# Waiting for a quarter of the input at a time in the first norm, and two bulk transfers issued ahead of the third layer norm

## What is computed

```python
x = hidden_states                                   # [16, 256, 128]
xn = layernorm(x)
s = L0_attn(xn)                                     # starts with an RMS norm of xn, then a gated linear recurrence and an MLP
g = silu(L0_ffn(xn))                                # two layers of local attention and feed-forward
x = x + s * g
xn = layernorm(x)                                   # "third layer norm": call 3 of the kernel
s = L1_attn(xn)                                     # 16 heads, ALiBi bias, causal
g = silu(L1_ffn(xn))                                # mixture of experts, 8 experts, each token goes to its best one
x = x + s * g
# two more layers of the same form: rope attention + ternary MLP, latent attention + linear map in the frequency domain

def L1_ffn(x):
    top1 = argmax(x @ Wg + bg)
    h = relu(x @ W1[top1] + b1[top1])
    return h @ W2[top1] + b2[top1]
```

## Time and profile before

| | |
|---|---|
| median of 3 runs | 2362.21 us (2360.13 to 2365.6) |
| the profiled execution | 2350.24 us, its span 2348.4 us |
| mean granted TensorE clock in it | 0.915 of full speed |
| PE busy | 1970.9 us, 84% of the span |
| DVE busy | 1403.9 us, 60% |
| ACT busy | 1173.3 us, 50% |
| POOL busy | 729.9 us, 31% |
| first matmul | 13.42 us |
| third layer norm | 1087.68 to 1126.95 us |
| alibi attention with routing | from 1126.95 us; the experts' first transfer is issued at 1394.29 |

### The profile page before, as it was taken

The page is one execution under the profiler, slowest core; times in us unless marked ns, Lnnn a source line. Parts: engine busy times, 40 slices in busy tenths (PEclk is TensorE's granted clock), DMA queues, the critical chain, the costliest instruction groups (busy, mean ns, idle before and its releaser), DMA issues. The chain is left out here.

```text
span 2348.4 us, 68942 instructions
## 1 busy us (share of the span) xinstructions
PE 1970.9 (84%) x28845; PEld 1250.0 (53%) x28845; DVE 1403.9 (60%) x2804; ACT 1173.3 (50%) x1869; POOL 729.9 (31%) x759
## 2 busy tenths in 40 slices
PE   5577899996959999787699989458998957999997
PEld 1232577763326777532555559325555414667765
DVE  5544788753568887255577735547775054556562
ACT  5663466654526666464366644325666441333333
POOL 0202666741057666201233103522220013222220
PEclk8787899998979999898699989759999987899999
DMA  3000000000000000000545520223441012433441
GB/s 136 0 0 1 2 3 3 3 3 1 0 1 3 3 3 3 2 0 5 160 121 128 137 60 28 77 57 95 98 99 43 0 41 91 133 124 119 139 127 39
DMA packets 93704, 122.43 MB, mean 52 GB/s; under 512 B 9376, under 2 KB 80384, under 8 KB 90048
## 3 DMA queue, kind: packets, MB, share of 16 engines
q1 hardware_dynamic: 91352, 113.84, 17.3%
q0 software_dynamic: 2048, 4.20, 0.6%
HBM read 67.62 MB, written 49.15 MB: 50 GB/s over the span
## 5 line engine op out<-in xcount | busy, mean ns | idle before, releaser
L1671 ACT ACTIVATE at_pr<-ps 128x768 f32<-128x768 f32 x256 | 203.9, 811 | 92.4 <-PE ps L1572 86.9
L1060 POOL TENSOR_TENSOR la_tc<-la_ta,la_tb 128x512 f32<-128x512 f32 x128 | 162.7, 1271 | 112.2 <-DVE la_tb L1356 108.2
L1077 PE MATMUL ps<-w_l0f,la_hs 128*128 128x512 f32 x256 | 152.7, 681 | 47.0 <-DVE la_tb L1356 40.7
L1996 ACT ACTIVATE at_pr<-ps 128x640 f32<-128x640 f32 x128 | 90.0, 703 | 179.4 <-PE ps L1899 179.4
L2038 DVE TENSOR_REDUCE at_m<-ps 128x2 f32<-128x512 f32 (+3 forms) x256 | 113.4, 485 | 105.7 <-PE ps L1899 102.1
L1716 DVE TENSOR_REDUCE at_m<-ps 128x2 f32<-128x512 f32 x256 | 174.2, 680 | 0.0
L2289 POOL TENSOR_TENSOR at_parts<-at_ta,at_tb 128x512 f32<-128x512 f32 x64 | 81.2, 1269 | 246.7 <-DVE at_tb L2279 242.7
L1047 POOL TENSOR_TENSOR la_qn<-la_tc,la_rn 128x512 f32<-128x512 f32 x128 | 133.9, 1046 | 52.9 <-issue 36.9
L1715 DVE TENSOR_REDUCE at_m<-ps 128x2 f32<-128x256 f32 x256 | 107.7, 421 | 67.2 <-PE ps L1572 62.7
L1572 PE MATMUL ps<-cast 64*64 64x256 bf16 x2048 | 146.3, 276 | 0.0
L1354 DVE TENSOR_TENSOR la_ta<-ps,la_tab 128x512 f32<-128x512 f32 x128 | 88.2, 689 | 95.7 <-ACT la_sq L1280 95.7
(11 more groups left out here) (380 smaller groups left out, 4872.9 us busy)
## 6 DMA issues: line engine op xcount, KB each, us to landing
scratch_latent<-at_parts SPq DMA_DIRECT2D x32, 640.0 KB
at_qs<-scratch_latent SPq DMA_DIRECT2D x32, 320.0 KB
at_ks<-scratch_latent SPq DMA_DIRECT2D x32, 320.0 KB
scratch_alibi<-at_parts SPq DMA_DIRECT2D x32, 192.0 KB
at_ks<-scratch_alibi SPq DMA_DIRECT2D x32, 192.0 KB
scratch_rope<-at_parts SPq DMA_DIRECT2D x32, 192.0 KB
at_ks<-scratch_rope SPq DMA_DIRECT2D x32, 192.0 KB
w_l0f<-in_l0f SPq DMA_DIRECT2D x2, 1689.5 KB, 15.6
```

Of the source, the lines that this page charges most:

```text
L1060: nc.gpsimd.tensor_tensor(tc[:, x, :], ta[:, x % 2, :], tb[:, x % 2, :], ALU.add).then_inc(s.la_tc, 1)
L1077: nc.tensor.matmul(ps[:, 0, :], hs[:, i % QSLOTS, t * P:(t + 1) * P], w("wq" if p < 2 else "wk"), start=True, stop=True).then_inc(s.la_pro ...
L1671: nc.scalar.activation(pr[:, p % RING, :, :], ps[:, at:at + 2, 0:384], ACT.Exp, scale=scale).then_inc(s.at_prob, 1)
```

## The change

In `double_norm` TensorE now waits by itself for `conf` and, ahead of each second tile, for the quarter of x with that tile. The load block no longer waits for x or for `cast`, and the cast moves from VectorE there to GpSimd in the norm's block (the argument `cast`). The clearing of `experts_in` and the load of `w_moe` leave the attention and are issued in the small block ahead of the third layer norm, behind the load of `w_l`; the zeroed tile is set by GpSimd in that block.

```diff
-def double_norm(k, call, rms_call, src, mid, dst, weight, ready):
+def double_norm(k, call, rms_call, src, mid, dst, weight, ready, cast):
...
+        @block.gpsimd
+        def _(pool):
+            pool.wait_ge(s.load_cast, 16)
+            nc.gpsimd.tensor_copy(*cast).then_inc(s.credit, 1)
+
         @block.tensor
         def _(pe):
             def centre(t):
+                if t == 0:
+                    pe.wait_ge(s.load_const, 16)
+                if t % 2 == 0:
+                    pe.wait_ge(s.load_x[t // 2], 16)
                 at_least(pe, s.ln_free, base + t + 1)
...
             for j, c, r in parts:
                 sp.dma_start(k.Y[r, 0:half], alibi[j][:, c * half:(c + 1) * half]).then_inc(s.alibi_loaded, 16)
-            g.sp_first(sp)
...
-    def sp_first(sp):
-        sp.wait_ge(s.moe_init, 2)
-        sp.dma_start(g.by_tile(g.sorted_in, 0, XT), zero[:].unsqueeze(1).to_broadcast([P, XT, P])).then_inc(s.moe_cleared, 16)
-    g.sp_first = sp_first
-
     def sp_step(sp, i, weights):
-        if i == 1:
-            sp.dma_start(k.w2b[:], weights[1]).then_inc(s.load_moe, 16)
         if i == B - 1:
             sp.wait_ge(s.moe_scattered, 16 * NCH)
-            sp.dma_start(k.Y[:], weights[0]).then_inc(s.load_moe, 16)
+            sp.dma_start(k.Y[:], weights).then_inc(s.load_moe, 16)
...
-            nc.gpsimd.memset(zero[:], 0.0).then_inc(s.moe_init, 1)
...
-                            sp.dma_start(k.X[:, cols], x[:, cols]).then_inc(s.load_x, 16)
-                        sp.dma_start(raw, cast).then_inc(s.load_const, 16)
+                            sp.dma_start(k.X[:, cols], x[:, cols]).then_inc(s.load_x[t], 16)
+                        sp.dma_start(raw, cast).then_inc(s.load_cast, 16)
...
-                        sp.wait_ge(s.load_x, 64)
...
-                        dve.wait_ge(s.load_const, 32)
-                        nc.vector.tensor_copy(castt[:], raw).then_inc(s.credit, 1)
...
             with nc.Block() as block:
+                @block.gpsimd
+                def _(pool):
+                    nc.gpsimd.memset(zero[:], 0.0).then_inc(s.moe_init, 1)
+
                 @block.sync
                 def _(sp):
                     sp.dma_start(t1[:], l1).then_inc(s.load_late, 16)
+                    sp.dma_start(k.w2b[:], moeb).then_inc(s.load_moe, 16)
+                    sp.wait_ge(s.moe_init, 1)
+                    sp.dma_start(k.by_tile(k.sorted_in, 0, XT), zero[:].unsqueeze(1).to_broadcast([P, XT, P])
+                                 ).then_inc(s.moe_cleared, 16)
                     sp.wait_ge(s.load_late, 16)
             layer_norm(k, 3, k.X, k.XN, gate=0)
```

More of the change, by code:

```diff
@@ L2373, in routing @@
     io = sb("io", [P, NEXP])
-    zero = sb("zero", [P, P])
     count_i = sb("counti", [P, XT], I32)
@@ L2810, in __init__ @@
     def __init__(self, new):
-        self.load_x = new("load_x")
+        self.load_x = [new(f"load_x{t}") for t in range(4)]
+        self.load_cast = new("load_cast")
         self.load_const = new("load_const")
@@ L3023, in program @@
                     work = [inner.enter_context(nc.sbuf_tensor(n, [P, N], F32)) for n in ("mix_h", "mix_gate")]
-                    double_norm(k, 0, 0, k.X, k.XN, work[0], w("norm"), ready=s.load_l0a)
+                    double_norm(k, 0, 0, k.X, k.XN, work[0], w("norm"), ready=s.load_l0a, cast=(castt[:], raw))
                     recurrent_mixer(k, w, work)
@@ L3045, in program @@
             k.w2b = inner.enter_context(nc.sbuf_tensor("w_moe", [P, W_MOEB[1]], F32))
+            zero = inner.enter_context(nc.sbuf_tensor("zero", [P, P], F32))
+            XT = N // P + NEXP - 1
+            k.sorted_in = nc.dram_tensor("experts_in", (XT * P, P), F32).ap()
+            k.by_tile = lambda dram, lo, hi: dram[lo * P:hi * P, :].rearrange("(t p) d -> p t d", p=P)
             with nc.Block() as block:
+                @block.gpsimd
+                def _(pool):
+                    nc.gpsimd.memset(zero[:], 0.0).then_inc(s.moe_init, 1)
                 @block.sync
```

5 lines of the change are left out of this document (2 added, 3 removed).

## The result

Eleven runs of each kernel: 2352.0 us median with the change (2345.87 to 2357.17), 2359.82 us without it (2352.92 to 2371.31). The ratio is 0.9965, 95% interval [0.9948, 0.9982]: 0.35% faster, some 8 us, with 4 to 12 us possible. The forecast was 12.0 us less and 2350.2 us.

The account below looks back on a forecast made before the run. The kernel was taken as stages separated by all-engine barriers, with transfer waits at two stage heads. Gains 7.0 + 5.0 = 12.0 us off the median 2362.21 gave 2350.2 us, range 2344 to 2357.5.

Parts of the forecast that it names:

- The start, 7.0 us: Load block and first norm: without waits for x and cast, TensorE starts at 6.4 instead of 13.42, 7.0 us earlier.
- the feared exclusion: First norm: GpSimd's cast could hold up VectorE operations with two SBUF inputs, costing 0 to 2.0 us; taken as 0.
- Rival (b): Start: first quarter of x or the cast is late, gaining 4.8 or 5.0 us instead of 7.0; 2352.3 us, chance 0.08.
- The issues ahead of the norm at no cost: Ahead of the third norm: two issues of 0.45 and 0.41 us fit before w_l lands, costing nothing, with 1.4 us cover.
- (d): Ahead of the third norm: clearing's issue held until w_moe lands, norm loses 9.8 us; 2360.0 us, chance 0.07.
- (e): Clearing's issue waits for w_moe and the block's end for the clearing: 21.4 us lost; 2371.6 us, chance 0.03.
- The attention, 5.0 us: Alibi attention's head: first scores wait for no transfer; at_xv is late next, so its matmuls start 5.0 us earlier.
- let the 5.0 us go through to the stage's end: Alibi attention: second and third row's loads taken as in time, so the whole 5.0 us reaches the stage's end.
- Rival (c): Alibi attention: TensorE, idle less and perhaps at higher clock, gains more, up to 8.7 us; 2346.5 us, chance 0.09.
- Rival (a): Only the start gains; the 5.0 us are given back within the attention; 2355.2 us, chance 0.17.

Follow-up runs that it names:

- the repeated pair: Kernels before and after the change, both unedited, run again on one chip: 2357.23 us (ratio 0.9991) and 2351.29 us (0.9954).
- e5_cast_x3: The changed kernel with the cast of the constants made three times on GpSimd instead of once: 2351.1 us, 0.997 of the kernel before.
- e12_cast_vector: The changed kernel with the cast on VectorE, at the head of its part of the norm's block: 2389.3 us, 0.9952 of the kernel before.
- e7_wl_last: The changed kernel with the load of w_l issued behind w_moe and the clearing: 2362.29 us, 1.0016 of the kernel before.
- e1_start_only: The change without its second half; clearing and w_moe stay in the alibi attention: 2388.55 us, 0.9966 of the kernel before.
- e2_attention_only: The change without its first half; clearing and w_moe ahead of the third norm, old start: 2389.63 us, 0.9966 of the kernel before.
- e6_xv_first: The changed kernel with GpSimd copying at_xv ahead of its rounds of the row: 2379.29 us, 0.9917 of the kernel before.
- e3_wmoe_back: The changed kernel with only the load of w_moe put back into the attention: 2384.25 us, 0.9948 of the kernel before.

## Why the prediction was right, and where a term was off

**The start, 7.0 us: right in mechanism, and in size for the pair shown.** First matmul 6.45 for 6.4, the quarters in time, the cast 1.57 us for 1.6, VectorE's first operation at 13.43 for 13.5 and its second at its normal length. The norm's end moved by 7.00, and by 7.3 in the repeated pair; over the seven profiles of the new start it is 6.6 on average. `e5_cast_x3` shows that the feared exclusion is real and `e12_cast_vector` that the old place on the engine wasn't the cost. Rival (b) is out as a cause: in no profile of the change did TensorE's first matmul wait for a quarter, or the cast meet a VectorE operation with two SBUF inputs; between the two lie 0.24 to 0.75 us. That the 6.4 came out to 0.05 us is in part luck. The sum was 6.02 for the last issue plus 0.4 for the barrier; measured are 5.86 plus 0.59, and the last issue alone moves by 0.7 us between profiles of the same code. The 0.4 had been taken from another barrier. The cast's 1.57 us is what the rows give: the slope between 0.40 and 0.613 us is 0.83 ns per element, not 0.85, and 0.40 + 1408 x 0.83 = 1.57.

**The issues ahead of the norm at no cost: right.** 0.43 and 0.42 us under the landing of `w_l`, 2.9 us for 2.6. `e7_wl_last` shows how much hangs on the order: the two transfers are free only behind the load that the barrier waits for. So (d) is out for this order. (e), that the queue passes the block's end only when the clearing has landed, is out by the norm's start at 1079.34, when the clearing had until 1076.94 + 16.5 = 1093.4 to land.

**The attention, 5.0 us: right at the wait, too large at the stage's end.** No transfer is waited for, L1542 waits for `at_xv` and starts 5.09 us earlier. The step that was mis-sized is "let the 5.0 us go through to the stage's end": 3.6 to 3.9 of them get there. The loss falls in the first two rows and has rows of the trace: after TensorE's 4.47 us idle its next products still run at the lower clock, 1.06 us where the same one took 0.60, and the lead is 4.3 us at the first row's maxima; in the second row's step the same scores take 0.53 us for 0.36, and the lead is 3.7. No run holds the clock fixed, so that the clock is all of the loss is read from these rows and not tested. Rival (c) had the sign of this wrong: the shorter idle time gave no higher clock there (L1542 took 1.19 us for 1.22). Rival (a), that all 5.0 would be given back, is out by the lead of 3.5 to 3.8 us that stays from the second row to the sixteenth in both pairs. The 3.9 us between the stages of `e1_start_only` and `e2_attention_only` agree, but on that chip lengths scatter by 3 us.

**The sum.** 7.0 + 3.8 = 10.8 instead of 12.0, and 10.4 with the start's average of 6.6. The two timings gave 8.3 us (4 to 12) and 10.9 (5 to 17), and agree with it; the first was nearer the low end, and 7.0 alone lies in both intervals, so it is the traces and the two halves and not the times that decide for both steps. The base was off too: 2362.21 over three runs, 2359.82 over eleven, 2.4 us too high. With that base and 10.8 us the forecast would have been 2349.0; with the 8.3 us that this timing showed it would have been 2351.5. Both errors are well inside the spread of 11 us that the eleven runs of the change have.

## What to carry to other kernels

Let a barrier wait only for what the next block's first instructions read, and give the rest to the instruction that needs it. Bulk transfers with slack go behind the small load that a barrier waits for, never ahead of it: the same three issues in another order took the whole gain back. When a wait goes, ask what is late next: here a copy that could itself be moved up, and with it the gain was 0.8% where the same kernel without it had 0.5% (`e6_xv_first` and `e12_cast_vector`, on one chip; their intervals just overlap). An operation that starts a few tenths of a microsecond later in one execution than in another can find the order between two engines turned round, so look at more than one profile of such a start. And where a change is worth less than 10 us of 2350, cut several profiles of each kernel at stage borders before blaming any stage.

## What the runs showed of the hardware

- An issue of a 264 KB load took 14.09 us when it stood behind a 2576 KB load and a 2496 KB clearing, while the clearing's own issue behind the load took 0.43.
- The clearing landed after 11.6 us in the attention, after 10.6 ahead of the norm without `w_moe` (`e3_wmoe_back`), and after 16.5 to 17.1 behind `w_moe`.
- A VectorE operation with two SBUF inputs took 1.95 and 1.82 us where a GpSimd cast was already running, and 0.69 with no GpSimd operation beside it; one with an input in PSUM kept its 0.69 beside the cast. Where the VectorE operation was first, it kept its 0.69 and the cast took 1.84 instead of 1.57.
- The first matmul behind the load block's barrier came 0.59 to 0.60 us after the queue's last issue in all seven profiles of that start, and that issue was over between 5.86 and 6.57.
- The same unchanged code, latent attention to the end, took 406.9, 411.3, 411.4 and 420.1 us in the four profiles of the two kernels; in the longest TensorE's granted clock was still at 0.50 from 60 to 80 us into the stage, where it was 0.83 in the shortest, with TensorE busy all the time in both.
- On two of the three chips the same kernel took 38 to 40 us more than the 2360 of the third. With the old attention the alibi stage was 298.4 us (`e1_start_only`) against 268.4 and 268.0, 30 of these us, with a granted clock of 0.91 from 1200 to 1300 where it was 1.00. Why, no run here tells.
